# Linear attention stage: epsilon as a column of the denominator sum, numerators in PSUM, and k and q added apart on GpSimd

## The chip, the cores and the metric

The kernel runs on one core of a Trainium2 chip. The metric is the device time of one execution in microseconds (us). The engines are TensorE (PE in the rows; PEld its weight loads), VectorE (DVE), ScalarE (ACT), GpSimd (POOL) and the DMA queues.

## The reference

One transformer layer on x of (16, 256, 128) float32: a causal linear attention with 16 heads of 8, and then a mixture of 16 experts (top 1) with a shared expert, each between layer norms and residual additions. The change touches the attention alone:

```
q = elu((x @ Wq + bq)) + 1;  k = elu((x @ Wk + bk)) + 1;  v = x @ Wv + bv     # x layer-normed
def step(carry, qkv):                     # over the 256 tokens of a row
    s, z = carry
    q_i, k_i, v_i = qkv
    s = s + jnp.einsum('bhd,bhm->bhdm', k_i, v_i)
    z = z + k_i
    qs = jnp.einsum('bhd,bhdm->bhm', q_i, s)
    qz = jnp.einsum('bhd,bhd->bh', q_i, z)[..., None]
    return ((s, z), qs / (qz + 1e-06))
return values @ Wo + bo
```

## The kernel before

The 4096 tokens are 32 tiles of 128 tokens, a token to a partition. A row of the batch is two tiles, an even one (the first half) and an odd one; what an odd tile needs of its even neighbour is the carried state. No loop runs on the chip: each engine's queue is written out by `step1(t, u)`, tile after tile, and `wait_ge` on counting semaphores ties the queues together. An engine takes its queue strictly in order, so a wait holds all that stands behind it.

For tile t, in the order of the data:

- TensorE transposes the normed x (L1032), ScalarE copies it to SBUF (`xnT`, L535), TensorE projects it to q, k and v in one PSUM bank (L1044), two tiles ahead: the queue of step t holds the projection of t + 2.
- ScalarE makes the halves of elu + 1: `neg` (L550), `rl` (L551), `ex` (L553), and copies v to `vv` (L555).
- GpSimd adds the halves, `qk <- ex, rl`, 128x256 for q and k together (L446), and multiplies k by v for every head, `kv`, 128x1024 (L452).
- TensorE sums k over the tokens up to each one with the triangular matrix `upto` (L1013, called z here); in even tiles it also makes the state to carry (L1017); and it sums `kv` in the same way into a pair of PSUM banks, `ps_s[u % 2]` (L1025: two halves of 512 columns, each two passes, so four rows in the trace). These sums of tile t may start when `kv` of t is there and VectorE's `prod` of t - 2 has read the same banks.
- VectorE multiplies q by the summed k (`zq`, L721) and q by the summed `kv` (`prod`, L735, 128x1024), reduces both over the 8 values of a head (`den` L752, `num` L757), adds epsilon to `den` (even tiles, L762; odd ones together with the carried part, L766), adds the carried numerators in odd tiles (L771), takes the reciprocal (L730) and multiplies (`att`, L745). The reciprocal and `att` of t - 1 stand in step t: the order of a step is zq(t), carry(t) if even, reciprocal(t-1), prod(t), att(t-1), den(t), num(t), and then L762, or L766 and L771.
- TensorE transposes `att` of t - 2 in step t (L1038), ScalarE copies it (`attT`, L545), TensorE multiplies it by Wo (L1051 for the bias and L1053), ScalarE stores it (L558). In odd tiles TensorE also transposes q (L1034), ScalarE copies it (`qT`, L541), and TensorE multiplies it by the carried state (L1058).

`s_chain` ("attention_steps") counts VectorE's operations of this stage, 6 for each tile (`CH`). `Z_READ` and `S_READ` say behind how many of them `zq` (and the carry) and `prod` are done. `s_att` counts the `att` tiles. From tile 28 on, VectorE places three small steps of the next stage's layer norms behind each of its attention steps (`other`).

Of the kernel before, what the change touches and what calls it, by code (L numbers as in the profile page):

```python
# [24 lines left out]
ALU = mybir.AluOpType  # L25
ACT = mybir.ActivationFunctionType
AX = mybir.AxisListType.X
# [110 lines left out]
def build(nc, x, w_att, b_qkv, bo, w_ffn, gate_up, down, out):  # L138
# [29 lines left out]
    with ExitStack() as ctx:  # L168
# [56 lines left out]
        zq = sb("zq", [P, D])  # L225
        den = sb("den", [P, NH])
        rden = sb("rden", [P, NH])
        prod = sb("prod", [P, KVW])
# [75 lines left out]
        s_bias_rows = sem("bias_rows_written")  # L304
        s_norm1 = sem("norm1_ready")
# [6 lines left out]
        s_v = sem("v_ready")  # L312
        s_qk = sem("qk_ready")
# [60 lines left out]
        CH = 6  # L374
# [53 lines left out]
        def _(pool):  # L428
# [7 lines left out]
            nc.gpsimd.memset(bias_rows[:], 0.0).then_inc(s_bias_clear, 1)  # L436
            nc.gpsimd.memset(rows[:, NT:ST, :], 0.0).then_inc(s_zero, 1)
# [4 lines left out]
            def step1(t, u):  # L442
# [3 lines left out]
                nc.gpsimd.tensor_tensor(qk[:, u, :], ex[:, u % 2, :], rl[:, u % 2, :], ALU.add).then_inc(s_qk, 1)  # L446
                pool.wait_ge(s_qk, t + 1)
# [5 lines left out]
                                        k, v, ALU.mult).then_inc(s_kv, 1)  # L453
            run_steps(pool, step1, 0, 4, 28, NT, 8, 4)
# [193 lines left out]
        def _(dve):  # L648
# [63 lines left out]
            def step1(t, u, others=iter(()), between=3):  # L712
# [4 lines left out]
                multiplied = S_READ[u % 2]  # L717
                if live(t, NT):

                    dve.wait_ge(s_z, t + 1)  # L720
                    nc.vector.tensor_tensor(zq[:], ps_qkv[u % 2][:, 3 * D:4 * D], qk[:, u, 0:D],  # L721
                                            ALU.mult).then_inc(s_chain, 1)
                    other()
# [4 lines left out]
                if live(t - 1, NT):  # L728
                    dve.wait_ge(s_chain, CH * (t - 1) + S_READ[1 - u % 2] + 3)
                    nc.vector.reciprocal(rden[:], rden[:]).then_inc(s_recip, 1)  # L730
                    other()
                if live(t, NT):
# [3 lines left out]
                        prod[:].rearrange("p (h m d) -> p h m d", h=NH, m=HD),  # L736
# [4 lines left out]
                if live(t - 1, NT):  # L741
                    dve.wait_ge(s_recip, t)
                    dve.wait_ge(s_chain, CH * t)
# [6 lines left out]
                if live(t, NT):  # L750
                    dve.wait_ge(s_chain, CH * t + Z_READ[u % 2])
                    nc.vector.tensor_reduce(den[:], zq[:].rearrange("p (h d) -> p h d", h=NH), AX,  # L752
                                            ALU.add).then_inc(s_chain, 1)
                    other()
                    dve.wait_ge(s_chain, CH * t + multiplied)
# [4 lines left out]
                    dve.wait_ge(s_chain, CH * t + multiplied + 1)  # L760
# [456 lines left out]
```

## Time and profile before

| what | us |
|---|---|
| median of 3 runs (342.65 to 344.68) | 344.0 |
| the profiled execution | 344.77 |
| its span | 342.8 |
| attention stage, from the first `zq` to the last `att` | 24.3 to 150.9 |
| busy in the span: PE, DVE, ACT, POOL | 269.8, 286.7, 186.5, 192.5 |

All rows below come from the one profiled execution. A row of the timeline gives the start from the beginning of the span, the duration, the engine, the line of the kernel, the operation and what it writes and reads; "x4" merges four of a kind, and in brackets stands how long the engine was idle before and who released it. A matmul's end is modelled, so on TensorE the distance from start to start says more than the duration.

### The profile page before, as it was taken

How to read it: one execution, taken by the hardware profiler on the slowest of the kernel's cores; microseconds unless marked ns; L12 is line 12 of the kernel's file. 1: busy time of each engine (PE TensorE's matmuls, PEld its weight loads, DVE VectorE, ACT ScalarE, POOL GpSimd, SP SyncE). 2: the span in 40 equal slices, each digit the busy share in tenths (PEclk: the TensorE clock that was granted, in tenths of full speed). 3: DMA queues.
4: the chain of work that ended last, by engine and by line, in shares of the span. 5: the costliest groups of instructions: out<-in, count | busy, mean ns of one | idle time of the engine just before them, and what ended most of it. 6: DMA issues, size and time to landing. Idle time of an engine off the chain costs nothing. (4 is left out here: it accounts for less than half of the span.)

```text
span 342.8 us, 6291 instructions
## 1 busy us (share of the span) xinstructions
PE 269.8 (79%) x1481; PEld 186.0 (54%) x1481; DVE 286.7 (84%) x1138; ACT 186.5 (54%) x573; POOL 192.5 (56%) x221
## 2 busy tenths in 40 slices
PE   3439999999998995839888888875999999998000
PEld 1215555555554552524555555543999888988000
DVE  6996999999999999996899988740389999999930
ACT  2524666656564652447666664203899888885000
POOL 5155777786776773300055556760007888888870
PEclk9987999999999999876999999999899999999755
DMA  6999900000000000000011111227940111110000
GB/s 190 376 424 391 409 8 0 2 3 0 2 0 2 2 0 0 0 2 2 0 63 64 63 62 64 95 78 238 354 158 24 31 35 37 40 36 30 26 2 0
DMA packets 13684, 28.39 MB, mean 83 GB/s; under 512 B 1966, under 2 KB 10166, under 8 KB 12626
## 3 DMA queue, kind: packets, MB, share of 16 engines
q1 hardware_dynamic: 10464, 21.57, 17.2%
q0 software_dynamic: 3040, 6.37, 5.5%
q8 instruction: 13, 0.21, 0.3%
q14 instruction: 21, 0.17, 0.2%
q10 hardware_dynamic: 146, 0.07, 0.1%
HBM read 15.38 MB, written 13.60 MB: 85 GB/s over the span
## 5 line engine op out<-in xcount | busy, mean ns | idle before, releaser
L452 POOL TENSOR_TENSOR kv<-qk,vv 128x1024 f32<-128x1024 f32 x32 | 62.4, 1950 | 2.5
L1025 PE MATMUL banks<-kv,upto 128*128 128x512 f32 x128 | 62.6, 612 | 1.3 <-POOL kv L452 1.3
L1164 PE MATMUL banks<-xsT,w_now 128*128 128x128 f32 x376 | 52.6, 284 | 0.3 <-DVE hT_e L964 0.3
L497 POOL DMA_INDIRECT out<-rows,token_i x47 | 46.8, 996 | 9.9 <-issue 8.3
L446 POOL TENSOR_TENSOR qk<-ex,rl 128x256 f32<-128x256 f32 x32 | 23.3, 727 | 47.2 <-ACT ex L553 47.2
L1164 PEld LDWEIGHTS banks<-xsT,w_now 128*128 128x128 f32 x376 | 47.1, 197 | 0.9 <-issue 0.6
L479 POOL DMA_INDIRECT sorted_rows<-rows,slot_i x32 | 31.7, 990 | 25.8 <-DVE slot_i L821 17.7
L735 DVE TENSOR_TENSOR prod<-banks,qk 128x1024 f32<-128x1024 f32 x32 | 38.9, 1216 | 3.5 <-PE banks L1025 2.9
L757 DVE TENSOR_REDUCE num<-prod 128x128 f32<-128x1024 f32 x32 | 38.6, 1207 | 0.3 <-DVE den L752 0.3
L964 DVE TENSOR_TENSOR hT_e<-silu_e,banks 128x256 f32<-128x256 f32 x47 | 19.3, 412 | 18.8 <-ACT silu_e L640 15.3
L1044 PE MATMUL banks<-w_qkvo,xnT 128*128 128x384 f32 x64 | 28.7, 532 | 8.1 <-ACT xnT L535 3.9
L491 POOL TENSOR_TENSOR rows<-rows,yn 128x128 f32<-128x128 f32 x40 | 19.0, 475 | 27.5 <-DVE yn L956 25.8
L1025 PEld LDWEIGHTS banks<-kv,upto 128*128 128x128 f32 x128 | 22.9, 198 | 17.6 <-issue 16.1
L1172 PE MATMUL banks<-w_exp_down,hT_e 128*128 x188 | 29.6, 280 | 1.0 <-DVE rows L981 1.0
L630 ACT ACTIVATE xs<-rows 128x128 f32<-128x128 f32 x47 | 23.2, 494 | 11.5 <-SPq L421 11.5
L644 ACT COPY w_now<-w_exp 128x512 f32 x47 | 28.7, 610 | 0.0
L535 ACT COPY xnT<-banks 128x128 f32<-128x128 f32 x32 | 8.5, 264 | 34.3 <-PE banks L1032 20.0
L1172 PEld LDWEIGHTS banks<-w_exp_down,hT_e 128*128 128x128 f32 x188 | 24.7, 191 | 1.5 <-issue 1.4
L640 ACT ACTIVATE silu_e<-banks 128x256 f32<-128x256 f32 x47 | 18.0, 383 | 11.8 <-PE banks L1164 11.1
L1120 PE MATMUL banks<-w_ffn,hT 128*128 128x128 f32 x128 | 16.4, 281 | 9.5 <-DVE hT L831 9.5
L528 ACT ACTIVATE xn<-rows,nm,rs 128x128 f32<-128x128 f32 x32 | 16.4, 517 | 10.3 <-DVE nm L122 10.3
L1120 PEld LDWEIGHTS banks<-w_ffn,hT 128*128 128x128 f32 x128 | 14.9, 191 | 11.2 <-DVE hT L831 11.2
(161 smaller groups left out, 647.8 us busy)
## 6 DMA issues: line engine op xcount, KB each, us to landing
sorted_rows<-rows SPq DMA_DIRECT2D x3, 1950.0 KB, 13.4
rows<-sorted_rows SPq DMA_DIRECT2D x10, 520.0 KB, 6.3
w_exp<-in_gate_up SPq DMA_DIRECT2D x4, 1024.0 KB, 20.3
w_exp_down<-in_down SPq DMA_DIRECT2D x4, 512.0 KB, 20.4
rows<-in_x SPq DMA_DIRECT2D x1, 1024.0 KB, 11.0
rows<-sorted_rows SPq DMA_DIRECT2D x2, 390.0 KB, 4.7
rows<-in_x SPq DMA_DIRECT2D x1, 768.0 KB, 8.2
out<-rows,token_i POOLq DMA_INDIRECT x47
```

Source lines behind the costliest of these rows:

```text
L446: nc.gpsimd.tensor_tensor(qk[:, u, :], ex[:, u % 2, :], rl[:, u % 2, :], ALU.add).then_inc(s_qk, 1)
L452: nc.gpsimd.tensor_tensor(kv[:, u, :].rearrange("p (h m d) -> p h m d", h=NH, m=HD), k, v, ALU.mult).then_inc(s_kv, 1)
L479: nc.gpsimd.indirect_dma_start(out=sorted_rows, out_offset=bass.IndirectOffsetOnAxis(ap=slot_i[:, t:t + 1], axis=0), in_=rows[:, t, :], in ...
L497: nc.gpsimd.indirect_dma_start(out=out_rows, out_offset=bass.IndirectOffsetOnAxis(ap=token_i[:, j - 1:j], axis=0), in_=rows[:, j - 1, 0:D] ...
L644: nc.scalar.copy(w_now[:, u % 2, :], flat(w_exp[:, bass.ds(e, 1), :])).then_inc(s_wn, 1)
L735: nc.vector.tensor_tensor(prod[:].rearrange("p (h m d) -> p h m d", h=NH, m=HD), ps_s[u % 2][:].rearrange("p (h m d) -> p h m d", h=NH, m=HD),
L757: nc.vector.tensor_reduce(num[:], prod[:].rearrange("p (n d) -> p n d", d=HD), AX, ALU.add).then_inc(s_chain, 1)
L1025: ins = nc.tensor.matmul(ps_s[u % 2][:, cols], upto[:], kv[:, u, cols], start=True, stop=True)
L1044: nc.tensor.matmul(ps_qkv[u % 2][:, 0:3 * D], xnT[:, u % 2, :], w_qkv, start=True, stop=True).then_inc(s_qkv, 1)
L1120: ins = nc.tensor.matmul(into, hT[:, f, k * P:(k + 1) * P], w_d[:, f, :], start=f == 0, stop=f == FC - 1)
L1164: ins = nc.tensor.matmul(ps_gue[u % 2][:, c * P:(c + 1) * P], w_now[:, u % 2, c * P:(c + 1) * P], xsT[:, u % 2, :], start=True, stop=True)
L1172: ins = nc.tensor.matmul(ps_ye[u % 2][:, 0:D], hT_e[:, u % 2, c * P:(c + 1) * P], flat(w_exp_down[:, bass.ds(e, 1), c, :]), start=c == 0, ...
```

## The change

- `zq` gets a ninth column for each head, which GpSimd fills once with epsilon, and two buffers. The reduction to `den` covers nine values, so L762 goes and L766 becomes a plain addition. There are now 5 counted VectorE operations in an even tile and 6 in an odd one (`steps_before`).
- The numerators are reduced into the first 128 columns of the tile's own pair of PSUM banks (even tiles), or written there by the addition of the carried part (odd tiles); `att` reads them from PSUM. `prod` gets two buffers.
- Since the banks now hold the numerators until `att` has read them, the sums of `kv` for tile t wait for `att` of t - 2 and no longer for `prod` of t - 2.
- GpSimd adds the k half of `qk` first, then multiplies `kv`, then adds the q half. The z sums and `kv` wait for the k half (`s_k`); `zq`, the transpose of q and ScalarE's `neg` of t + 2 wait for the q half (`s_qk`).

```diff
-        CH = 6
+        def steps_before(t):
+            return 11 * (t // 2) + 5 * (t % 2)
...
+            nc.gpsimd.memset(zq[:, :, :, HD:HD + 1], EPS_DEN).then_inc(s_eps, 1)
...
-                nc.gpsimd.tensor_tensor(qk[:, u, :], ex[:, u % 2, :], rl[:, u % 2, :], ALU.add).then_inc(s_qk, 1)
-                pool.wait_ge(s_qk, t + 1)
+                nc.gpsimd.tensor_tensor(qk[:, u, D:2 * D], ex[:, u % 2, D:2 * D], rl[:, u % 2, D:2 * D], ALU.add
+                                        ).then_inc(s_k, 1)
+                pool.wait_ge(s_k, t + 1)
...
                 nc.gpsimd.tensor_tensor(kv[:, u, :].rearrange("p (h m d) -> p h m d", h=NH, m=HD),
                                         k, v, ALU.mult).then_inc(s_kv, 1)
+                nc.gpsimd.tensor_tensor(qk[:, u, 0:D], ex[:, u % 2, 0:D], rl[:, u % 2, 0:D], ALU.add).then_inc(s_qk, 1)
...
+                summed, summed_last = ps_s[u % 2][:, 0:D], ps_s[1 - u % 2][:, 0:D]
...
                     dve.wait_ge(s_z, t + 1)
+                    dve.wait_ge(s_qk, t + 1)
...
                     nc.vector.tensor_tensor(att[:, 1 - u % 2, :].rearrange("p (h m) -> p h m", h=NH),
-                                            num[:].rearrange("p (h m) -> p h m", h=NH),
+                                            summed_last.rearrange("p (h m) -> p h m", h=NH),
...
-                    nc.vector.tensor_reduce(num[:], prod[:].rearrange("p (n d) -> p n d", d=HD), AX,
+                    nc.vector.tensor_reduce(num[:] if u % 2 else summed, prod[:, u % 2, :].rearrange("p (n d) -> p n d", d=HD), AX,
...
-                    if u % 2 == 0:
-                        nc.vector.tensor_scalar(rden[:], den[:], EPS_DEN, None, ALU.add).then_inc(s_chain, 1)
+                    if u % 2:
...
+                        nc.vector.tensor_tensor(rden[:], ps_xT[:, 3 * D:2 * D + CW], den[:], ALU.add).then_inc(s_chain, 1)
...
-                        nc.vector.tensor_tensor(num[:], num[:], ps_xT[:, 2 * D:3 * D], ALU.add).then_inc(s_chain, 1)
+                        nc.vector.tensor_tensor(summed, num[:], ps_xT[:, 2 * D:3 * D], ALU.add).then_inc(s_chain, 1)
...
                     pe.wait_ge(s_kv, t + 1)
-                    at_least(pe, s_chain, CH * (t - 2) + S_READ[odd])
+                    at_least(pe, s_att, t - 1)
```

VectorE's queue over an even and then an odd tile, before (banks2 and banks4 are the two pairs for the sums, banks0 holds the z sums, banks6 the carried part):

```order
L745 TENSOR_TENSOR att<-num,rden 128x128 [waits att_transposed,attention_steps,denominator_inverted]
L752 TENSOR_REDUCE den<-zq 128x16 [waits attention_steps]
L757 TENSOR_REDUCE num<-prod 128x128 [waits att_ready,attention_steps]
L762 TENSOR_SCALAR rden<-den 128x16 [waits attention_steps]
L721 TENSOR_TENSOR zq<-banks0,qk 128x128 [waits z_summed]
L730 RECIPROCAL rden<-rden 128x16 [waits attention_steps]
L735 TENSOR_TENSOR prod<-banks4,qk 128x1024 [waits state_summed]
```

And after, the same place:

```order
L756 TENSOR_TENSOR att<-banks4,rden 128x128 [waits att_transposed,attention_steps,denominator_inverted]
L765 TENSOR_REDUCE den<-zq 128x16 [waits attention_steps]
L770 TENSOR_REDUCE banks2<-prod 128x128 [waits att_ready,attention_steps]
L730 TENSOR_TENSOR zq<-banks0,qk 128x16x8 [waits qk_ready,z_summed]
L741 RECIPROCAL rden<-den 128x16 [waits attention_steps]
L746 TENSOR_TENSOR prod<-banks4,qk 128x1024 [waits state_summed]
```

The epsilon operation is gone, `att` reads and the reduction writes PSUM, and `zq` has one more wait.

TensorE's queue from the sums of an even tile to those of the next odd one, before:

```order
L1025 MATMUL banks<-kv,upto 128x512 [waits attention_steps,kv_ready]
L1025 MATMUL banks<-kv,upto 128x512
L1032 MATMUL banks<-ident,xn 128x128 [waits xnT_ready,xn_ready,attention_steps]
L1038 MATMUL banks<-ident,att 128x128 [waits y_stored,att_ready]
L1044 MATMUL banks<-w_qkvo,xnT 128x384 [waits attention_steps,xnT_ready]
L1051 MATMUL banks<-bias_rows,ones_bf 128x128 [waits attT_ready]
L1053 MATMUL banks<-w_qkvo,attT 128x128
L1013 MATMUL banks<-qk,upto 128x128 [waits v_ready,qk_ready]
L1025 MATMUL banks<-kv,upto 128x512 [waits attention_steps,kv_ready]
```

And after:

```order
L1033 MATMUL banks<-kv,upto 128x512 [waits att_ready,kv_ready]
L1033 MATMUL banks<-kv,upto 128x512
L1040 MATMUL banks<-ident,xn 128x128 [waits xnT_ready,xn_ready,attention_steps]
L1047 MATMUL banks<-ident,att 128x128 [waits y_stored,att_ready]
L1053 MATMUL banks<-w_qkvo,xnT 128x384 [waits attention_steps,xnT_ready]
L1060 MATMUL banks<-bias_rows,ones_bf 128x128 [waits attT_ready]
L1062 MATMUL banks<-w_qkvo,attT 128x128
L1021 MATMUL banks<-qk,upto 128x128 [waits v_ready,k_ready]
L1033 MATMUL banks<-kv,upto 128x512 [waits att_ready,kv_ready]
```

Nothing changes place; the sums wait for `att` in place of a step of the chain, and z for the k half alone.

GpSimd's queue for two tiles, before and after:

```order
L446 TENSOR_TENSOR qk<-ex,rl 128x256 [waits elu_halves_ready]
L452 TENSOR_TENSOR kv<-qk,vv 128x1024 [waits v_ready,qk_ready]
L446 TENSOR_TENSOR qk<-ex,rl 128x256 [waits elu_halves_ready]
L452 TENSOR_TENSOR kv<-qk,vv 128x1024 [waits v_ready,qk_ready]
L446 TENSOR_TENSOR qk<-ex,rl 128x256 [waits elu_halves_ready]
```

```order
L451 TENSOR_TENSOR qk<-ex,rl 128x128 [waits elu_halves_ready]
L458 TENSOR_TENSOR kv<-qk,vv 128x1024 [waits v_ready,k_ready]
L460 TENSOR_TENSOR qk<-ex,rl 128x128
L451 TENSOR_TENSOR qk<-ex,rl 128x128 [waits elu_halves_ready]
L458 TENSOR_TENSOR kv<-qk,vv 128x1024 [waits v_ready,k_ready]
L460 TENSOR_TENSOR qk<-ex,rl 128x128
```

Two operations a tile become three, with the q half behind `kv`.

## Rows read from the trace of the kernel before

**Rows 1.** Windows: stretch, length, busy PE, PEld, DVE, ACT, POOL, granted clock, DMA.

```profile
60.00:100.00 40.00, 39.92 (x177) 23.03 (x177) 39.72 (x92) 24.86 (x98) 29.79 (x24) 1.00 0.01 1
```

**Rows 2.** Timeline of VectorE: `zq` of four odd tiles.

```profile
36.83 0.28 DVE L721 TENSOR_TENSOR zq<-banks,qk 128x128 f32<-128x128 f32 x1
...
100.53 0.28 DVE L721 TENSOR_TENSOR zq<-banks,qk 128x128 f32<-128x128 f32 x1
...
109.47 0.28 DVE L721 TENSOR_TENSOR zq<-banks,qk 128x128 f32<-128x128 f32 x1
...
116.32 0.28 DVE L721 TENSOR_TENSOR zq<-banks,qk 128x128 f32<-128x128 f32 x1
```

**Rows 3.** Timeline of TensorE over one pair of tiles.

```profile
100.74 0.27 PE L1032 MATMUL banks<-ident,xn 128*128 128x128 f32 x1
...
101.89 0.10 PEld L1051 LDWEIGHTS banks<-bias_rows,ones_bf 128*128 128x128 bf16 x1 [0.63 <-ACT attT L545]
...
102.95 1.88 PE L1025 MATMUL banks<-kv,upto 128*128 128x512 f32 x4
...
104.67 0.27 PE L1032 MATMUL banks<-ident,xn 128*128 128x128 f32 x1
...
106.09 1.88 PE L1025 MATMUL banks<-kv,upto 128*128 128x512 f32 x4
```

**Rows 4.** Timeline of VectorE over the same pair and the next step.

```profile
100.46 0.17 DVE L762 TENSOR_SCALAR rden<-den 128x16 f32<-128x16 f32 x1
...
100.94 1.22 DVE L735 TENSOR_TENSOR prod<-banks,qk 128x1024 f32<-128x1024 f32 x1
...
102.08 0.52 DVE L745 TENSOR_TENSOR att<-num,rden 128x128 f32<-128x128 f32 x1
...
104.57 0.24 DVE L730 RECIPROCAL rden<-rden 128x16 f32<-128x16 f32 x1
104.87 1.23 DVE L735 TENSOR_TENSOR prod<-banks,qk 128x1024 f32<-128x1024 f32 x1
...
106.01 0.28 DVE L745 TENSOR_TENSOR att<-num,rden 128x128 f32<-128x128 f32 x1
...
107.89 1.67 DVE L762 TENSOR_SCALAR rden<-den 128x16 f32<-128x16 f32 x1
```

**Rows 5.** Timeline of GpSimd over the same stretch: `kv`.

```profile
100.50 1.95 POOL L452 TENSOR_TENSOR kv<-qk,vv 128x1024 f32<-128x1024 f32 x1
...
103.76 1.95 POOL L452 TENSOR_TENSOR kv<-qk,vv 128x1024 f32<-128x1024 f32 x1
...
107.58 1.95 POOL L452 TENSOR_TENSOR kv<-qk,vv 128x1024 f32<-128x1024 f32 x1
```

**Rows 6.** Timeline at the end of the stage, GpSimd and VectorE.

```profile
131.00 1.95 POOL L452 TENSOR_TENSOR kv<-qk,vv 128x1024 f32<-128x1024 f32 x1
131.09 2.02 DVE L745 TENSOR_TENSOR att<-num,rden 128x128 f32<-128x128 f32 x1
```

**Rows 7.** One line each: ns min/median/max, first and last start.

```profile
L721 DVE TENSOR_TENSOR zq<-banks,qk x32: 276/283/292, 24.3 to 147.1; 128x128 f32<-128x128 f32 x32
L745 DVE TENSOR_TENSOR att<-num,rden x32: 272/282/2015, 31.6 to 150.6; 128x128 f32<-128x128 f32 x32
L446 POOL TENSOR_TENSOR qk<-ex,rl x32: 722/727/732, 16.2 to 138.0; 128x256 f32<-128x256 f32 x32
```

**Rows 8.** Timeline of the start: GpSimd, VectorE and TensorE.

```profile
16.97 1.95 POOL L452 TENSOR_TENSOR kv<-qk,vv 128x1024 f32<-128x1024 f32 x1
17.44 1.54 DVE L93 TENSOR_TENSOR scratch<-stats 128x28 f32<-128x28 f32 x1
...
18.97 1.98 PE L1025 MATMUL banks<-kv,upto 128*128 128x512 f32 x4 [1.29 <-POOL kv L452]
...
20.79 0.27 PE L1032 MATMUL banks<-ident,xn 128*128 128x128 f32 x1
```

**Rows 9.** One line: a 128x128 addition on GpSimd in a later stage.

```profile
L491 POOL TENSOR_TENSOR rows<-rows,yn x40: 442/477/502, 255.4 to 322.8; 128x128 f32<-128x128 f32 x40
```

More of the change, by code:

```diff
@@ L224, in build @@
         kv = sb("kv", [P, 4, KVW])
-        zq = sb("zq", [P, D])
+        zq = sb("zq", [P, 2, NH, HD + 1])
         den = sb("den", [P, NH])
         rden = sb("rden", [P, NH])
-        prod = sb("prod", [P, KVW])
+        prod = sb("prod", [P, 2, KVW])
         num = sb("num", [P, D])
@@ L304, in build @@
         s_bias_rows = sem("bias_rows_written")
+        s_eps = sem("denominator_eps_written")
         s_norm1 = sem("norm1_ready")
@@ L312, in build @@
         s_v = sem("v_ready")
+        s_k = sem("k_ready")
         s_qk = sem("qk_ready")
@@ L728, in step1 @@
                 if live(t - 1, NT):
-                    dve.wait_ge(s_chain, CH * (t - 1) + S_READ[1 - u % 2] + 3)
-                    nc.vector.reciprocal(rden[:], rden[:]).then_inc(s_recip, 1)
+                    dve.wait_ge(s_chain, steps_before(t - 1) + (4 if u % 2 else 5))
+                    nc.vector.reciprocal(rden[:], (den if u % 2 else rden)[:]).then_inc(s_recip, 1)
                     other()
@@ L735, in step1 @@
                     nc.vector.tensor_tensor(
-                        prod[:].rearrange("p (h m d) -> p h m d", h=NH, m=HD),
+                        prod[:, u % 2, :].rearrange("p (h m d) -> p h m d", h=NH, m=HD),
                         ps_s[u % 2][:].rearrange("p (h m d) -> p h m d", h=NH, m=HD),
@@ L750, in step1 @@
                 if live(t, NT):
-                    dve.wait_ge(s_chain, CH * t + Z_READ[u % 2])
-                    nc.vector.tensor_reduce(den[:], zq[:].rearrange("p (h d) -> p h d", h=NH), AX,
+                    dve.wait_ge(s_chain, steps_before(t) + Z_READ[u % 2])
+                    if t == 0:
+                        dve.wait_ge(s_eps, 1)
+                    nc.vector.tensor_reduce(den[:], zq[:, u % 2, :, :], AX,
                                             ALU.add).then_inc(s_chain, 1)
@@ L763, in step1 @@
                         other()
-                    else:
-                        dve.wait_ge(s_carried, t + 1)
-                        nc.vector.scalar_tensor_tensor(out=rden[:], in0=den[:], scalar=EPS_DEN,
-                                                       in1=ps_xT[:, 3 * D:2 * D + CW],
-                                                       op0=ALU.add, op1=ALU.add).then_inc(s_chain, 1)
-                        other()
-                        dve.wait_ge(s_chain, CH * t + multiplied + 2)
-                        nc.vector.tensor_tensor(num[:], num[:], ps_xT[:, 2 * D:3 * D], ALU.add).then_inc(s_chain, 1)
+                        dve.wait_ge(s_chain, steps_before(t) + multiplied + 2)
@@ L1007, in step1 @@
                 if live(t, NT):
-                    pe.wait_ge(s_qk, t + 1)
+                    pe.wait_ge(s_k, t + 1)
                     pe.wait_ge(s_v, t + 1)
@@ L1033, in step1 @@
                 if odd and live(t, NT):
+                    pe.wait_ge(s_qk, t + 1)
                     nc.tensor.transpose(ps_xT[:, D:2 * D], qk[:, u, 0:D], ident[:]).then_inc(s_q_t, 2)
@@ L1042, in step1 @@
                         pe.wait_ge(s_folded, 1)
-                    at_least(pe, s_chain, CH * t + Z_READ[odd])
+                    at_least(pe, s_chain, steps_before(t) + Z_READ[odd])
                     nc.tensor.matmul(ps_qkv[u % 2][:, 0:3 * D], xnT[:, u % 2, :], w_qkv,
@@ L1130, in _ @@
             pe.wait_ge(s_xnT, NT)
-            pe.wait_ge(s_chain, CH * NT)
+            pe.wait_ge(s_chain, steps_before(NT))
             step2(-1, 1)
-            pe.wait_ge(s_chain, CH * NT)
+            pe.wait_ge(s_chain, steps_before(NT))
             pe.wait_ge(s_y_out, NT)
```

15 lines of the change are left out of this document (9 added, 6 removed).

## The prediction

> **What bounds the kernel now.** I first cut the span into stretches and read each engine's busy time and the granted clock [rows 1]. From 60 to 100 us, the middle of the attention stage, TensorE is busy 39.92 of 40 us and VectorE 39.72 of 40, at the full granted clock (1.00, which is 2.4 GHz). Busy shares can't tell two full engines apart, so the timeline of one pair of tiles comes next: the program repeats every two tiles, an odd one and an even one. The odd `zq` starts at 36.83 and at 100.53 us, nine pairs later [rows 2]: 7.08 us for a pair.
>
> On TensorE [rows 3] the pair beginning at 100.74 is: transposes and the rest of the odd step until the k v sums (L1025, below "the sums") of the even tile start at 102.95, 2.21 us; their four passes until 104.67, 1.72; transposes, projection, output, z until the odd tile's sums at 106.09, 1.42; four passes until 107.81, 1.72. Sum 7.07 (the second four passes taken like the first). The only hole is a small one before L1051 at 101.89, whose row names `attT` of ScalarE. TensorE never waits for VectorE in this pair.
>
> VectorE's own row [rows 4]: the even `prod` starts at 104.87, 0.04 us behind the end of the sums (102.95 + 1.88). The step from the reciprocal (104.57, 0.24 long) to it is 0.30, while operations here start some 0.08 ahead of the end of the one before (`prod` 100.94 + 1.22 = 102.16, `att` 102.08), so that 0.16 to 0.2 would do. So VectorE waits about 0.1 us a pair for TensorE. Inside the pair it also loses 0.24: the odd `att` takes 0.52 instead of 0.28, and ends when GpSimd's `kv` (100.50 + 1.95 = 102.45) is through [rows 4, 5]. Since the pair's length is TensorE's, these 0.24 us are no loss of the kernel now; without them the 0.1 wait would be 0.34. That reading decides the forecast.
>
> Two stalls are different in kind, because they are too long to be absorbed. At 107.89 the 128x16 add of epsilon (L762), else 0.17 us long, takes 1.67: it begins 0.31 behind a `kv`, while at 100.46 it begins 0.04 ahead of one [rows 4, 5]. A short pause of VectorE just before had made it late. The pair is 8.94 long instead of 7.07 and the next 6.85 [rows 2]: net 1.65 us lost. At 131.09 `att` takes 2.02 behind a `kv` of 131.00 [rows 6]; VectorE is the bound there, since the norm steps of the next stage stand between the attention steps.
>
> **The change part by part.**
>
> *Epsilon.* 16 adds L762 leave VectorE. Start to start each costs 0.07 (100.46 to 100.53) [rows 4], 14 of them in steps paced by TensorE: nothing. Two (tiles 28 and 30) lie where VectorE is the bound: -0.14 at most. L766 becomes a plain add, equal. The `den` reduction reads 144 values instead of 128: with `att` 0.28 for 128 and `prod` 1.22 for 1024 [rows 4] about 1 ns a value, +0.02, hidden by VectorE's idle time. `zq` is now written in runs of 8 with a gap; no row shows such a write. Bounds 0 and +0.1, I take 0; at +0.1 it is hidden too. The held L762 at 107.89 is gone: **-1.65**, bounds -1.87 and -1.5. The memset of the column is 32 values on GpSimd at 1.8 us, far ahead of its first tile (its `kv` at 16.97): 0.
>
> *Numerators in PSUM.* `att` then has one SBUF input. The row shows that `att` with both inputs in SBUF is held behind `kv`; no operation with a PSUM input is (`zq` at 276 to 292 ns in all 32 cases, the one at 100.53 during a `kv`) [rows 2, 5, 7]. So the odd `att` falls from 0.52 to 0.28: off the path, 0. A PSUM write by VectorE is in no row; a PSUM input costs nothing visible (`zq` 283 against `att` 282 ns, medians) [rows 7]. For the write I bound 0 to +0.1 each, take 0; in the even step it falls into the time that VectorE idles anyway.
>
> The Trainium skill, "VectorE: DVE Perf Modes", section on the TRN2 errata, speaks against this: it gives a fixed 120 cycles for a PSUM source against 58 for SBUF, so `att` would be some 0.065 us longer (an estimate from that page), and 13 of them on the path below would add 0.8 us. The rows of this case (283 against 282 ns) do not show it, and I leave it out.
>
> *The wait that this brings.* The numerators of tile t-2 lie in the banks into which the sums of tile t go. The sums used to wait for `prod` of t-2; now they wait for `att` of t-2, which VectorE does only behind `prod` of t-1. Even tile: `att` (odd step) starts 102.08, would end 102.36, the sums start 102.95: free. Odd tile: `att` starts at 106.01 and ends at 106.29, but the sums start at 106.09 [rows 3, 4]. They must move behind it. How much an engine needs from a release: at the first tile the sums start at 18.97, 0.05 behind the end of `kv` (16.97 + 1.95), and the next instruction on TensorE starts 1.82 later instead of 1.72, since the weights are not loaded ahead [rows 8]. So the effective start is 106.29 + 0.05 + 0.10 = 106.44, **+0.35 a pair**. Bounds: +0.20 (no latency at all) and +0.38. Does something give it back? Everything behind the sums on TensorE's queue (transposes of xn, q and att, projection of tile t+2, then ScalarE's copies and the q, k, v of that tile) moves with them. `att` can't come earlier: it is `prod` (1.14) behind the end of the even sums, and these are TensorE's. The even half keeps 3.93 us (1.72 + 2.21). The new pair is 1.92 + 1.14 + 0.28 + 0.15 + 3.93 = 7.42. VectorE needs about 7.07 - 0.1 - 0.24 - 0.07 = 6.66 and waits. The odd tiles from 3 to 27 are 13: +4.55.
>
> *The halves on GpSimd.* k (128x128) is about 0.48 (the 128x128 add of L491) [rows 9] instead of the 0.73 of the whole `qk` [rows 7]: `kv` is ready 0.25 earlier. TensorE had the odd `kv` (103.76 + 1.95 = 105.71) 0.38 before it used it (106.09) [rows 3, 5], so nothing is won. q comes 0.56 behind `kv`, at about 106.0 here (105.71 - 0.25 + 0.56), for a `zq` of that tile which starts behind the L762 of 107.89; the transpose of q stands behind the sums in TensorE's queue, and ScalarE asks for q later still (its L550). GpSimd's queue becomes 0.48 + 1.95 + 0.48 + two gaps of 0.08 = 3.1 us a tile where the pair leaves 3.54 (7.07 / 2): it fits. 0. If q were late, `zq` and the projection behind it would be, at 0.1 a tile for each 0.1.
>
> *Start.* The norm chain of 28 tiles (L93 to L122) has small operations with two SBUF inputs, held while GpSimd works (L93 1.54 us behind the `kv` of 16.97) [rows 8]; ScalarE waits for its end. The first `kv` begins 0.25 earlier, but two more adds can hold a step. -0.2, bounds -0.5 and +0.5.
>
> *End of the stage, 127 to 151 us.* VectorE is the bound. It comes 0.2 earlier relative to TensorE. `att` at 131.09 is no longer held, but the norm steps L108 and L110 right behind it have two SBUF inputs and stand before the same `kv`: the first of them is held instead, so of 1.74 only some 0.3 is won. Together with the two L762: **-0.6**, bounds -2.2 (all 1.74 saved) and +1.5 (another small step held by a `kv`).
>
> *Sum.* +4.55 - 1.65 - 0.2 - 0.6 = +2.1. The profiled execution took 344.8 (span 342.8), 0.8 above the median 344.0 of the three; I read that as the held L762, which need not occur in each. The sum against the profiled one is 346.9, and the changed kernel has no such event, so its median should lie at it: **346.8 us**.
>
> **Rivals.**
> 1. *VectorE paces the pair* (0.14). For: 99% busy, its wait of 0.1 us is small and TensorE's ends are modelled. Then each pair gives back 0.24 + 0.07, 13 pairs 4.0, the two long stalls 3.4 and the start 0.2: 337.2. Against: TensorE has no hole in which it waits for VectorE [rows 3]. The Trainium skill, "SBUF — State Buffer", section on the two separate sides, states an exclusive lock between a VectorE operation with two SBUF inputs and a GpSimd operation; the held rows agree, and by it every attention step is freed. It is this rival's mechanism, but says nothing on who paces.
> 2. *The new wait costs its lower bound and the end its best* (0.24): 13 x 0.20 = 2.6, -1.65 - 2.2 - 0.2: 343.3; with 0.35 and the same end 345.3. No measurable change.
> 3. *More is held* (0.12): the small norm steps at start or end meet two further `kv`, 1.7 us each: 350.3; with one 348.6.
> 4. My forecast, sums behind `att`: 0.50, 346.0 to 347.6.
>
> That the change doesn't free `att` at all would alter little, since those 0.24 us are off the path.
>
> **How the numbers follow.** The other side of the forecast is rival 1, which decides if the sums of odd tiles turn out to start no later relative to `att` of the step before than now. 0.5% is 1.7 us, about what a measurement here can tell: faster means below 342.3, slower above 345.7. Faster: 0.14 and a quarter of rival 2, 0.20. Slower: 0.12 and most of 0.50, 0.54. Same: 0.26. Range 339.5 to 349.5; it leaves out the core of rival 1 and the far end of rival 3.
>
> **What the changed profile would show.** The odd `zq` 7.4 us apart (rival 1: 6.8 to 6.9); the first pass of the odd sums some 0.05 to 0.15 behind the end of `att`, with `att` as releaser; before `prod` some 0.3 to 0.4 us idle on VectorE; every `att` at 0.28; no long operation between 36 and 125 us; and around 131 us one L106, L108 or L110 held for 1.5 us or more. I am wrong if the pair stays at 7.07, if VectorE has no idle time in it, or if a PSUM write costs tenths of a us.

## The result, and the profile after

The changed kernel takes 350.5 us (median of four runs, 348.2 to 351.3) against 344.05 (342.65 to 344.68, four runs): ratio 1.018, interval 1.012 to 1.024. That is 6.4 us slower. The forecast was 346.8, 2.8 us slower. Its direction was right, its size was not, and 350.5 lies 1 us outside the range. The profiled execution took 348.18 (span 346.4, mean granted clock 0.935), the shortest of the four; the others took 349.97 to 351.29 at 0.909 to 0.930. All comparisons of traces below are of profiled executions, 348.18 against 344.77.

The middle of the attention stage first, by windows (columns as in [rows 1]):

```profile
60.00:100.00 40.00, 38.99 (x168) 22.43 (x169) 36.38 (x84) 23.60 (x91) 29.86 (x33) 1.00 0.00 1
```

TensorE was busy 39.92 of 40 us and is at 38.99, VectorE went from 39.72 to 36.38: both have holes now. The timeline of one pair shows where (start, us, engine, line, operation; in brackets the idle time before it and its releaser). The sums, L1025 of before, are L1033 here, `att` is L756, `prod` L746, `zq` L730, `kv` L458 and the two halves of `qk` L451 (k) and L460 (q).

```profile
61.06 1.88 PE L1033 MATMUL banks<-kv,upto 128*128 128x512 f32 x4
...
62.98 1.22 DVE L746 TENSOR_TENSOR prod<-banks,qk 128x1024 f32<-128x1024 f32 x1 [0.27 <-PE banks L1033]
...
64.12 0.28 DVE L756 TENSOR_TENSOR att<-banks,rden 128x128 f32<-128x128 f32 x1
...
64.52 0.30 PEld L1033 LDWEIGHTS banks<-kv,upto 128*128 128x128 f32 x2 [0.35 <-issue]
64.55 1.96 PE L1033 MATMUL banks<-kv,upto 128*128 128x512 f32 x4 [0.18 <-DVE att L756]
...
65.66 0.28 DVE L730 TENSOR_TENSOR zq<-banks,qk 128x128 f32<-128x128 f32 x1
...
66.34 0.27 PE L1040 MATMUL banks<-ident,xn 128*128 128x128 f32 x1
66.54 1.22 DVE L746 TENSOR_TENSOR prod<-banks,qk 128x1024 f32<-128x1024 f32 x1 [0.45 <-PE banks L1033]
...
73.15 0.28 DVE L730 TENSOR_TENSOR zq<-banks,qk 128x128 f32<-128x128 f32 x1
```

These answer to [rows 2 to 4]. The odd `zq` starts at 65.66 and 73.15: 7.49 us a pair, where it was 7.07. The even sums end at 62.94, `prod` starts 0.04 later, `att` ends at 64.40, and the odd sums, which before started 0.08 behind the *start* of `att`, now load their weights 0.12 behind its *end* and name it as releaser. VectorE idles 0.27 and 0.45 before its two `prod`, since everything on TensorE has moved back.

Over the whole stage, by groups of instructions of the page (busy us, mean ns | idle us before them, and what ended it):

```profile
L1033 PE MATMUL banks<-kv,upto 128*128 128x512 f32 x128 | 67.3, 652 | 9.4 <-DVE att L756 8.5
...
L746 DVE TENSOR_TENSOR prod<-banks,qk 128x1024 f32<-128x1024 f32 x32 | 39.1, 1223 | 11.9 <-PE banks L1033 11.9
```

Before, the same two lines of the page read

```profile
L1025 PE MATMUL banks<-kv,upto 128*128 128x512 f32 x128 | 62.6, 612 | 1.3 <-POOL kv L452 1.3
...
L735 DVE TENSOR_TENSOR prod<-banks,qk 128x1024 f32<-128x1024 f32 x32 | 38.9, 1216 | 3.5 <-PE banks L1025 2.9
```

8.5 us of waiting for `att` are new, and the sums themselves are 4.7 us longer in all (67.3 against 62.6). About 1 us of the second is the 1.96 against 1.88 of the sums that wait in the middle; most of the rest lies at the end of the stage. Timeline of the changed kernel there, VectorE, GpSimd and the sums:

```profile
131.60 1.22 DVE L746 TENSOR_TENSOR prod<-banks,qk 128x1024 f32<-128x1024 f32 x1
...
133.19 1.96 POOL L458 TENSOR_TENSOR kv<-qk,vv 128x1024 f32<-128x1024 f32 x1
133.36 1.80 DVE L106 TENSOR_TENSOR scratch<-scratch 128x4 f32<-128x4 f32 x1
135.09 0.28 DVE L756 TENSOR_TENSOR att<-banks,rden 128x128 f32<-128x128 f32 x1
...
135.51 3.75 PE L1033 MATMUL banks<-kv,upto 128*128 128x512 f32 x4 [3.37 <-DVE att L756]
...
139.30 1.23 DVE L746 TENSOR_TENSOR prod<-banks,qk 128x1024 f32<-128x1024 f32 x1 [1.16 <-PE banks L1033]
...
148.12 3.48 PE L1033 MATMUL banks<-kv,upto 128*128 128x512 f32 x4 [3.13 <-DVE att L756]
```

and the windows of that place in the changed kernel, TensorE's granted clock being the column before the last two:

```profile
134.00:141.00 7.00, 5.49 (x10) 2.54 (x11) 5.70 (x16) 0.43 (x2) 1.55 (x2) 0.51 0.00 0
```

The norm step L106 is held behind a `kv`, as the prediction said some such step would be. But `att` of tile 27 is queued right behind it, and the sums of tile 29 now wait for that `att`. TensorE stands still for 3.37 us, and then its four passes take 3.75 instead of 1.88: the granted clock is 0.51, so 1.2 GHz, the lower of its two levels. The same happens again at 148.12 for tile 31, where the residual addition L880 (1.91 us from 143.49) and further steps of the next stage stand ahead of `att`. Before, the sums of tile 29 ran at 129.52 in 1.88 us, ahead of the held `att` of [rows 6]. The granted clock falls at the end of the stage before the change too (0.76 over the same 134 to 141 us, 0.60 from 135.7 to 138.7), where TensorE has had 0.44 us of work in 4.3 us (131.4 to 135.7); what is new is that two tiles' sums run inside the low clock from their start and that VectorE waits for the first of them: `prod` at 139.30 has 1.16 us of idle time ahead of it.

Marks along the stage, in us of the two profiled executions:

| | before | after | difference |
|---|---|---|---|
| `zq` of tile 0 | 24.32 | 24.27 | -0.05 |
| `zq` of tile 3 | 36.83 | 35.69 | -1.14 |
| tile 3 to tile 27 (12 pairs) | 86.56 | 89.90 | +3.34 |
| tile 27 to tile 31 | 23.69 | 25.56 | +1.87 |
| tile 31 to the end of the last `att` | 3.84 | 4.05 | +0.21 |
| rest of the span | 191.9 | 191.2 | -0.7 |

The -1.14 can't be put down to the change: between 20 and 36 us the granted clock was 0.79 in one and 1.00 in the other, and among the kernels below (apart from "halves alone", whose add is held there) tile 3 starts at 34.9 to 37.4 without a pattern. The rest of the span, which is identical code, lies between 190.5 and 194.8 in the profiles of all kernels below.

### The profile page after: what moved, and what is told of

The parts are those of the page before. It is cut to its first block and busy times, and to the rows that moved or that the text cites. A ratio compares the mean times of both kernels' runs of the same rounds, so it can differ in the third digit from the quotient of the medians.

```text
span 346.4 us, 6357 instructions
## 1 busy us (share of the span) xinstructions
PE 276.8 (80%) x1481; PEld 187.8 (54%) x1481; DVE 282.3 (81%) x1122; ACT 186.2 (54%) x573; POOL 197.5 (57%) x254
## 5 line engine op out<-in xcount | busy, mean ns | idle before, releaser
L1033 PE MATMUL banks<-kv,upto 128*128 128x512 f32 x128 | 67.3, 652 | 9.4 <-DVE att L756 8.5
L458 POOL TENSOR_TENSOR kv<-qk,vv 128x1024 f32<-128x1024 f32 x32 | 62.4, 1951 | 2.5
L746 DVE TENSOR_TENSOR prod<-banks,qk 128x1024 f32<-128x1024 f32 x32 | 39.1, 1223 | 11.9 <-PE banks L1033 11.9
L451 POOL TENSOR_TENSOR qk<-ex,rl 128x128 f32<-128x128 f32 x32 | 14.5, 454 | 46.8 <-ACT ex L560 46.8
L1033 PEld LDWEIGHTS banks<-kv,upto 128*128 128x128 f32 x128 | 23.8, 206 | 29.6 <-issue 25.0
L964 DVE TENSOR_SCALAR yn<-rows,rstd,nmean 128x128 f32<-128x128 f32 x47 | 19.8, 420 | 0.0
```

Source lines behind the costliest of these rows:

```text
L458: nc.gpsimd.tensor_tensor(kv[:, u, :].rearrange("p (h m d) -> p h m d", h=NH, m=HD), k, v, ALU.mult).then_inc(s_kv, 1)
L746: nc.vector.tensor_tensor(prod[:, u % 2, :].rearrange("p (h m d) -> p h m d", h=NH, m=HD), ps_s[u % 2][:].rearrange("p (h m d) -> p h m d" ...
L964: nc.vector.tensor_scalar(yn[:, u, :], flat(rows[:, i, D:2 * D]), rstd3[:, parity, u:u + 1], nmean3[:, parity, u:u + 1], ALU.mult, ALU.add ...
L1033: ins = nc.tensor.matmul(ps_s[u % 2][:, cols], upto[:], kv[:, u, cols], start=True, stop=True)
```

## The experiments

The theory after the result: the sums' new wait for `att` of tile t-2 costs all of the loss, 0.42 us a pair and about 2 us at the end of the stage; epsilon column, PSUM as a place for numerators, and the halves on GpSimd add nothing to it. Rivals: the PSUM operands are slow; the halves on GpSimd delay something; the end is late for another reason. "Middle" is `zq` of tile 3 to tile 27, "end" is tile 27 to tile 31, both from the profiled execution. The medians stand against the kernel before as it ran on the same chip beside them: 343.58 (first four kernels), 344.23 (next four), 344.02 (last four).

| kernel | median us | ratio, interval | pair | middle | end |
|---|---|---|---|---|---|
| before | 344.05 | 1 | 7.07 | 86.56 | 23.69 |
| changed | 350.49 | 1.018, 1.012 to 1.024 | 7.49 | 89.90 | 25.56 |
| wait alone | 349.82 | 1.021, 1.011 to 1.030 | 7.49 | 91.12 | 25.52 |
| passes of the sums swapped | 343.38 | 0.997, 0.992 to 1.001 | 7.07 | 85.13 | 23.92 |
| numerators in SBUF | 343.54 | 1.001, 0.998 to 1.005 | 7.07 | 85.12 | 23.31 |
| qk whole | 350.21 | 1.019, 1.011 to 1.026 | 7.49 | 89.90 | 24.91 |
| last tiles in SBUF | 347.08 | 1.008, 1.004 to 1.012 | 7.49 | 89.90 | 24.47 |
| swapped, last in SBUF | 342.31 | 0.995, 0.991 to 0.999 | 7.07 | 85.11 | 24.05 |
| epsilon column alone | 343.33 | 0.997, 0.993 to 1.001 | 7.09 | 85.52 | 23.53 |
| halves alone | 361.55 | 1.048, 1.039 to 1.057 | 8.44 | 101.51 | 23.90 |
| attT first, before | 343.92 | 0.999, 0.995 to 1.002 | 7.07 | 86.47 | 24.36 |
| attT first, changed | 346.42 | 1.007, 1.003 to 1.010 | 7.32 | 87.93 | 25.57 |
| attT first, numerators in SBUF | 339.52 | 0.985, 0.980 to 0.990 | 6.90 | 83.15 | 23.33 |
| attT first, swapped, last in SBUF | 340.52 | 0.988, 0.983 to 0.993 | 6.90 | 83.25 | 24.04 |

**The wait alone**, put into the kernel before, where it is not needed (the numerators are in SBUF there):

```diff
-                    at_least(pe, s_chain, CH * (t - 2) + S_READ[odd])
+                    at_least(pe, s_att, t - 1)
```

> The kernel before with one line changed: TensorE's sums of tile t wait for att of t-2 instead of prod of t-2; everything else, numerators in SBUF and the epsilon step included, stays. Theory (the new wait is what costs): the pair of tiles goes from 7.07 to about 7.49 us as in the changed kernel, VectorE idles before prod, and the time is 348 to 352. At the end of the stage the sums of tile 29 wait behind the held att and the clock falls, as in the changed kernel. Rival (PSUM operands or the halves of GpSimd cost): pair within 0.05 of 7.07 and time within 1 us of before.

Measured +6.2 us, the same as the whole change within the intervals. Its rows in the timeline read like those of the changed kernel:

```profile
64.22 0.28 DVE L745 TENSOR_TENSOR att<-num,rden 128x128 f32<-128x128 f32 x1
64.65 1.96 PE L1025 MATMUL banks<-kv,upto 128*128 128x512 f32 x4 [0.19 <-DVE att L745]
```

and so does its end: L106 held for 1.80, 25.52 us from tile 27 to 31. Neither PSUM nor the halves are in this kernel, so neither is needed for the loss. One thing was not expected: `att` has both inputs in SBUF and yet always takes 0.28 in the middle. The wait has shifted VectorE against GpSimd: the `att` that was held before begins at 67.78 here, and the `kv` ahead of it (65.79 + 1.95) is over at 67.74. One L762 is held here too (at 111.03, 1.68), which makes the middle 91.12.

**The passes of the sums swapped.** The numerators lie in the first bank of a pair of banks. So the second half of the sums can go first, under the old wait, and only the first half waits for `att`:

```diff
-                    at_least(pe, s_att, t - 1)
-                    for half in range(2):
+                    at_least(pe, s_chain, steps_before(t - 2) + S_READ[odd] if t >= 2 else 0)
+                    for half in (1, 0):
+                        if half == 0:
+                            at_least(pe, s_att, t - 1)
```

> The changed kernel with the two halves of the sums in the other order: the half whose bank holds no numerators is summed first and waits only for prod of t-2, the other half waits for att of t-2. Theory (wait): the first half (0.86 us) covers the end of att, which came 0.2 us behind the old start; pair back to 7.05 to 7.10; no TensorE idle in front of the sums between 36 and 125 us; 345 or less; the end of the stage still pays. Rival: pair stays at 7.4 to 7.5.

The loss is gone and the pair is back at 7.07. The sums (L1035 here) start 0.08 behind the start of `att`, without a wait, while the numerators are still written to PSUM and read from there:

```profile
63.51 0.28 DVE L756 TENSOR_TENSOR att<-banks,rden 128x128 f32<-128x128 f32 x1
63.59 1.88 PE L1035 MATMUL banks<-kv,upto 128*128 128x512 f32 x4
```

That rules out the PSUM operands as a cost: everything of the change but the position of the wait is in this kernel.

A miss: I expected the end still to pay, and it takes 23.92, as before the change. L106 is held for the same 1.80 (at 129.07), and TensorE still waits for the `att` behind it, but with half of the sums already done:

```profile
131.12 1.12 PE L1035 MATMUL banks<-kv,upto 128*128 128x512 f32 x2 [2.42 <-DVE att L756]
```

The half that is left takes 1.12 us, and the next `prod` finds it finished.

**Numerators in SBUF**, with the old wait, and the rest of the change kept:

```diff
-                summed, summed_last = ps_s[u % 2][:, 0:D], ps_s[1 - u % 2][:, 0:D]
+                summed, summed_last = num[:], num[:]
...
-                    at_least(pe, s_att, t - 1)
+                    at_least(pe, s_chain, steps_before(t - 2) + S_READ[odd] if t >= 2 else 0)
```

> The changed kernel with the numerators back in SBUF and the sums waiting for prod of t-2 again; the epsilon column and GpSimd's halves stay. Theory (wait): pair 7.05 to 7.10, odd att held again to about 0.5 us, no held step at 107.89 since L762 is gone; total 342 to 344. Rival (halves or epsilon column cost): pair above 7.2.

The time is that of before. A miss: I expected the odd `att` to be held again, at some 0.5. It takes 0.28. With the half of k alone ahead of it, `kv` starts earlier: 0.54 behind the even sums (67.23 and 66.69), where it was 0.81 (103.76 and 102.95 in [rows 3, 5]). The `kv` that used to hold `att` is nearly over when `att` begins:

```profile
60.16 1.95 POOL L458 TENSOR_TENSOR kv<-qk,vv 128x1024 f32<-128x1024 f32 x1
...
62.68 0.28 DVE L756 TENSOR_TENSOR att<-num,rden 128x128 f32<-128x128 f32 x1
...
63.98 1.95 POOL L458 TENSOR_TENSOR kv<-qk,vv 128x1024 f32<-128x1024 f32 x1
65.82 0.28 DVE L756 TENSOR_TENSOR att<-num,rden 128x128 f32<-128x128 f32 x1
```

The one at 65.82 is the odd `att`: 0.11 us of the `kv` of 63.98 (until 65.93) are left, where 0.37 were left in [rows 4, 5] (102.45 less 102.08). Against the changed kernel this one is 7.0 us faster by the medians; the traces give 4.8 in the middle and 2.25 at the end, together 7.0. So the price of the wait is known in both places.

**qk whole**, one addition of q and k ahead of `kv` again, the rest as changed:

```diff
-                nc.gpsimd.tensor_tensor(qk[:, u, D:2 * D], ex[:, u % 2, D:2 * D], rl[:, u % 2, D:2 * D], ALU.add
-                                        ).then_inc(s_k, 1)
+                nc.gpsimd.tensor_tensor(qk[:, u, :], ex[:, u % 2, :], rl[:, u % 2, :], ALU.add).then_inc(s_qk, 1)
...
-                nc.gpsimd.tensor_tensor(qk[:, u, 0:D], ex[:, u % 2, 0:D], rl[:, u % 2, 0:D], ALU.add).then_inc(s_qk, 1)
...
-                    pe.wait_ge(s_k, t + 1)
+                    pe.wait_ge(s_qk, t + 1)
```

> The changed kernel with qk added whole ahead of kv, as before; epsilon column and numerators in PSUM stay. Theory (wait): pair 7.45 to 7.5 as in the changed kernel, since kv is not what TensorE waits for; total within 1.5 us of the changed kernel. Rival (the halves cost): pair falls below 7.3.

Same time, same pair as the changed kernel, and at the end the same picture: L106 held for 1.80, sums of 3.64 us behind it, `prod` 1.19 us late. (The end is 24.91 and not 25.56; its L878, the L880 of the changed kernel, takes 1.09 instead of 1.91.) The halves are not what costs here.

**The last tiles in SBUF.** Tiles from 26 on keep their numerators in SBUF, and the sums of tiles 28 to 31 have the old wait:

```diff
+                summed = ps_s[u % 2][:, 0:D] if t < 26 else num[:]
...
-                    at_least(pe, s_att, t - 1)
+                    if t - 2 < 26:
+                        at_least(pe, s_att, t - 1)
+                    else:
+                        at_least(pe, s_chain, steps_before(t - 2) + S_READ[odd])
```

> The changed kernel, but tiles 26 to 31 keep their numerators in SBUF and the sums of tiles 28 to 31 wait for prod of t-2 as before. Theory (the second part of the loss is the same wait where VectorE is the bound: att of 27 stands behind a held norm step, TensorE idles 3.4 us and its clock halves): pairs 7.49 up to 125 us, then from the zq of tile 27 to that of 31 23.3 to 23.9 us instead of 25.56, total about 2 us below the changed kernel, 348 to 349. Rival (the end is slower for another reason): still 25 or more.

The middle is unchanged to the hundredth. L106 is held just the same, but no sums stand behind it now (timeline of this kernel):

```profile
131.22 1.88 PE L1037 MATMUL banks<-kv,upto 128*128 128x512 f32 x4
132.61 1.80 DVE L106 TENSOR_TENSOR scratch<-scratch 128x4 f32<-128x4 f32 x1
134.34 0.28 DVE L757 TENSOR_TENSOR att<-num,rden 128x128 f32<-128x128 f32 x1
```

They run ahead of the held step and in 1.88 us, and over 134 to 141 us the granted clock is 0.76, as in the kernel before, where the changed one has 0.51:

```profile
134.00:141.00 7.00, 3.83 (x13) 2.84 (x14) 6.38 (x19) 2.11 (x8) 1.66 (x4) 0.76 0.00 0
```

The end takes 24.47, 1.1 less than in the changed kernel but more than the 23.3 to 23.9 expected. By medians 3.4 us are won (2 expected), but a gain of 1.1 is at the edge of what the two intervals allow, so scatter can account for the difference. Of the 1.2 us that its end is longer than in "numerators in SBUF", 0.4 lies in the first pair (12.24 against 11.81): the sums of tile 27 wait for tile 25, which this kernel still keeps in PSUM. What the rest consists of was not settled.

**Both remedies together**, swapped passes and the last tiles in SBUF:

> Both remedies: halves of the sums in the other order and SBUF numerators from tile 26 on. Theory: pair 7.07, end 23.3 to 23.9, total 342.5 to 343.5, a little below the kernel before because no epsilon step can be held. Rival: above 344.

342.3 us, 0.5% under before, pair 7.07. Its end (24.05) is a little above the 23.3 to 23.9 expected and no better than with the swap alone (23.92).

**The epsilon column alone**, in the kernel before (nothing in PSUM, qk whole):

> The kernel before with the epsilon column alone: qk whole, numerators in SBUF, sums wait for prod. Theory: pair 7.07, since TensorE paces it; the odd att is held to 0.5 us as before; no held epsilon step; 342.5 to 344. Rival (the column pays for itself on VectorE): pair 6.9 or below.

No measurable difference, no held add, pair 7.08 to 7.10. With qk whole and numerators in SBUF the odd `att` is held again, and at the end of the stage it meets a whole `kv`:

```profile
64.91 1.95 POOL L457 TENSOR_TENSOR kv<-qk,vv 128x1024 f32<-128x1024 f32 x1
66.48 0.53 DVE L754 TENSOR_TENSOR att<-num,rden 128x128 f32<-128x128 f32 x1
```

Beside "numerators in SBUF", which differs from this kernel only in the halves, this separates the two causes: the half of k, by starting `kv` 0.27 earlier, is enough to free `att` of its hold; PSUM operands are not needed for it.

**The halves alone**, in the kernel before, with its 16 adds of epsilon (L766 here):

> The kernel before with GpSimd's halves alone: k half, kv, q half; epsilon step, SBUF numerators and the old wait stay. Following the timeline, kv then starts 0.25 us earlier relative to ScalarE and the epsilon step (0.04 ahead of kv before) starts behind it and is held up to 1.8 us in every even tile: pair about 8.4 and total about 360. Rival (the order on GpSimd does not matter as long as TensorE paces): pair 7.07, total 343 to 345.

361.6 us, 17 more than before. `kv` begins earlier, and so just ahead of an add that used to slip in before it:

```profile
61.75 1.95 POOL L454 TENSOR_TENSOR kv<-qk,vv 128x1024 f32<-128x1024 f32 x1
61.97 1.75 DVE L766 TENSOR_SCALAR rden<-den 128x16 f32<-128x16 f32 x1
...
70.40 1.95 POOL L454 TENSOR_TENSOR kv<-qk,vv 128x1024 f32<-128x1024 f32 x1
70.44 1.94 DVE L766 TENSOR_SCALAR rden<-den 128x16 f32<-128x16 f32 x1
```

Each even tile now loses it: 8.44 us a pair, as the expectation had it, and 8.66 in the one pair that holds the add of 70.44. In [rows 4, 5] the add began 0.04 ahead of `kv` and took 0.17; here at 70.44 it begins 0.04 behind and takes 1.94. By themselves the halves are the dearest part of the change; in this kernel they can only be had together with the epsilon column, which removes that add.

**attT first.** The last four kernels look for what else bounds the pair. ScalarE copies `qT` ahead of `attT` in odd tiles, and TensorE has its only regular hole where it waits for `attT` [rows 3]. The two blocks are exchanged, without any other edit:

```diff
-                if u % 2 and live(t, NT):
-                    act.wait_ge(s_q_t, t + 1)
-                    at_least(act, s_carried, t - 1)
-                    nc.scalar.copy(qT[:], ps_xT[:, D:2 * D]).then_inc(s_qT, 2)
                 if live(t - 2, NT):
                     act.wait_ge(s_att_t, t - 1)
                     at_least(act, s_y, t - 2)
                     nc.scalar.copy(attT[:], ps_o[:, 0:D]).then_inc(s_attT, 1)
+                if u % 2 and live(t, NT):
+                    act.wait_ge(s_q_t, t + 1)
+                    at_least(act, s_carried, t - 1)
+                    nc.scalar.copy(qT[:], ps_xT[:, D:2 * D]).then_inc(s_qT, 2)
```

> The kernel before with ScalarE's two copies of odd tiles in the other order: attT ahead of qT. TensorE's only hole in a pair, about 0.19 us in front of the output product, waits for attT. Theory (TensorE paces): the hole shrinks by up to 0.16 and the pair to 6.9, but with its held odd att VectorE needs 6.97, so it ends at 6.95 to 7.0 and VectorE becomes the bound: 341.5 to 343.5. Rival (TensorE is not the pace): 7.07 stays.

A miss: on the kernel before it changes nothing. The hole did shrink, from 5.4 us in 60 to 100 us to 3.6 (groups of that stretch, before and then this kernel):

```profile
L1051 PEld LDWEIGHTS banks<-bias_rows,ones_bf 128*128 128x128 bf16 x11 | 1.1, 95 | 5.4 <-ACT attT L545 5.4
```

```profile
L1051 PEld LDWEIGHTS banks<-bias_rows,ones_bf 128*128 128x128 bf16 x11 | 1.0, 95 | 3.6 <-ACT attT L541 3.6
```

But a delay of the same size has appeared in the even step (timeline of this kernel):

```profile
61.29 0.30 DVE L726 TENSOR_TENSOR carry<-banks,head_mask 128x144 f32<-128x144 f32 x1
...
61.73 0.88 PE L1044 MATMUL banks<-w_qkvo,xnT 128*128 128x384 f32 x2
...
64.93 1.23 DVE L735 TENSOR_TENSOR prod<-banks,qk 128x1024 f32<-128x1024 f32 x1
66.07 0.52 DVE L745 TENSOR_TENSOR att<-num,rden 128x128 f32<-128x128 f32 x1
```

The projection L1044 may start only when VectorE's `carry` is done, since both touch the same banks. Here `carry` ends at 61.59 and L1044 starts at 61.73, 0.31 behind L1032 and 0.88 long; in the kernel before it ends at 104.66, L1044 starts at 104.89, 0.22 behind L1032, and is 0.81 long. So there is a second path of the pair that goes through both engines: `carry`, L1044, the odd sums, the odd `prod` (64.93, 0.04 behind the sums), the held odd `att`, and the rest of VectorE's step up to the next `carry`. It is as long as TensorE's own, 7.07, and with the hole made smaller it sets the pair. The 0.24 us of the held `att` lie on it. So before the change the two paths were equal to less than 0.1 us, and a gain on TensorE alone brings nothing.

The same exchange in the changed kernel, where VectorE has 0.7 us of idle time a pair:

> The changed kernel with the same swap on ScalarE. The path of its pair (even sums, prod, att, odd sums, the odd half of TensorE) goes through the hole, so theory: 7.49 - 0.16 = 7.33, and 2 us less in all, 347.5 to 349. Rival (the pair is set by something beside that path): 7.49 stays.

7.32 a pair and 4.1 us less than the changed kernel by the medians; the traces show 2.0 of them, in the middle, and 2.0 was expected. The two intervals allow both. Here TensorE and the wait set the pair, no `att` is held, and the hole on TensorE counts.

And with the numerators in SBUF, halves and epsilon column kept:

> Numerators in SBUF with the old wait, epsilon column, halves of qk, and attT ahead of qT. In that kernel no att was held in the pairs, so VectorE needs about 6.66: theory pair 6.90 to 6.93, total 341 to 342, below the kernel before by 0.6 to 0.9%. Rival: att gets held again since the pair is shorter, 7.0 or more.

339.5 us, 4.5 less than before and 11 less than the changed kernel: the lowest of all, with a pair of 6.90. With both remedies in place of the numerators in SBUF it is 340.5, the same pair and 0.7 more at the end; the two intervals overlap:

> Halves of the sums in the other order, SBUF numerators from tile 26 on, epsilon column, halves of qk, and attT ahead of qT: pair 6.90 to 6.93; total 340.5 to 341.5, below the kernel before and the changed kernel. Rival: no shorter than 7.07.

In no kernel here does PSUM as a place for the numerators bring anything that SBUF does not.

## Why the prediction was wrong in size

*What held.* TensorE paces the pair, not VectorE (rival 1: 6.8 to 6.9 a pair; it is 7.49). The even sums run free, the odd ones wait for `att`, with it as releaser. `prod` waits 0.27 and 0.45 (said: 0.3 to 0.4). Every `att` takes 0.28; no long operation lies between 36 us and the end of the middle, so the held L762 of 107.89 is gone. L106 is held at the end. The halves add nothing to the cost (whole qk: 350.2), and an operation of VectorE into or out of PSUM costs nothing that counts: the reduction of 1024 takes 1.22 us into PSUM and 1.21 into SBUF, `att` from PSUM 281 ns where it was 282 from SBUF. The Trainium skill, "VectorE: DVE Perf Modes", errata section, gives a PSUM source a higher fixed cost than an SBUF source; I had left that out of the sum, and these rows do not show it. One reading was luckier than it looks: that the held `att` is off the path is true only because a second path, with it, is no longer than TensorE's own ("attT first").

*Term 1, the wait, +0.35 a pair: +0.42.* I took 0.05 as the time from a release to the sums, from one row of the start, where they wait for GpSimd, plus 0.10 for weights not loaded ahead. Measured: `att` ends at 64.40, the weights load at 64.52, and L1040 starts at 66.34, which with 1.72 us of passes is a start at 64.62. That is 0.22 behind the end of `att` instead of 0.15, and beyond my upper bound of +0.38. Over the twelve pairs of the middle it makes +0.8.

*Term 2, the end of the stage, -0.6, or -0.25 with the wait of the thirteenth pair, which lies there: +2.1* (1.87 + 0.21 of the marks). This is the step that failed. I followed `att` into the place where VectorE is the bound, said that a norm step would be held there instead, and priced it at what VectorE saves. I did not carry the new wait there. In the middle, the wait costs what TensorE loses against an `att` that is on time; at the end `att` stands behind 1.8 us of held norm step, and the sums, which before went ahead of all that, stand behind `att`. TensorE does nothing for 3.4 us, the granted clock behind that is 0.51, and the late sums take twice their time. The kernel with the wait alone has the same end (25.52), the one with numerators in SBUF has 23.31 although its L106 is held for the same 1.80: so it is the wait and not the held step. No run separates waiting from clock within the 2.25, but rows give an estimate. In "numerators in SBUF" `prod` of tile 29 follows its `zq` at once, and L880 is shorter:

```profile
132.70 0.28 DVE L730 TENSOR_TENSOR zq<-banks,qk 128x128 f32<-128x128 f32 x1
...
133.05 1.16 DVE L746 TENSOR_TENSOR prod<-banks,qk 128x1024 f32<-128x1024 f32 x1
...
137.18 1.26 DVE L880 TENSOR_TENSOR rows<-rows,ya 128x256 f32<-128x256 f32 x2
```

In the changed kernel `zq` starts at 137.70 and `prod`, held up for 1.16, at 139.30. Sums of 1.96 us from 135.51 would have ended at 137.47, ahead of that `zq`. So by this estimate the 1.16 us are there because the sums ran at the low clock: about half of the 2.25. Another 0.65 is L880 (1.91 against 1.26, each beside a `kv`; 1.09 to 1.91 in the kernels with the wait), and 0.30 the first pair (12.11 against 11.81). My upper bound of +1.5 thought of another held step and not of this.

*Term 3, the start, -0.2.* `zq` of tile 0 came 0.05 earlier, within the bounds. The norm chain went as followed: L93 at 17.67 held for 1.27 instead of 1.54.

*Term 4, from the sum to the median.* +2.1 on the profiled 344.77 gave 346.9; the profiled execution of the changed kernel is 348.18, 1.3 more: +0.8 and +2.3 by the two terms above, less 1.0 at the start, 0.7 in the rest of the span and 0.2 outside of it (1.2, and 0.1 of rounding). Its median is another 2.3 higher. I had set a sum made against one profiled execution equal to a median, with the reason that the held L762 (-1.65) was what put it above its own. That credit does not show clearly in the medians: the kernels without the wait and without the held add ("passes swapped", "numerators in SBUF", "epsilon column alone") lie at 343.3 to 343.5 against 343.6 and 344.2 of before, a gain of 0.0 to 0.9, while their traces are 1.2, 1.8 and 1.2 shorter in middle and end together. For two of the three the interval has room for the 1.2; for "numerators in SBUF" (0.998 to 1.005) it has none for 1.8. That the add is rarely held is not likely: the other two traces of kernels in which it stands at its old place hold it too, in the same pair ("wait alone" at 111.03 for 1.68, "attT first, before" at 107.05 for 1.85). What gives the credit back stays open. Without it the sum at the median would be +7.0 for the wait, less a few tenths, and the result is +6.4.

*The chances.* The rival that the end is worse (3, held norm steps, 348.6 or 350.3) came nearest in time, for another reason than it gave.

## What to carry to other kernels

When a result is put into the buffer that the next producer writes, the producer waits for the last reader instead of the first: price that wait in each stage apart, above all where the reader's engine is the bound and has other work queued ahead of it. If the buffer has parts, let the producer do the free part first: exchanging the two halves gave back all 7 us here. And where two paths are within 0.1 us of each other, shortening one brings nothing (attT first: 0) until the other is shorter as well (numerators in SBUF with attT first: 6.90 a pair instead of 7.07, 4.5 us under before).

## What the runs showed of the hardware

- From the end of an operation of VectorE to the load of weights that waits for it 0.12 us; until the waiting matmuls are effectively under way 0.22 (64.40, 64.52, 64.62 in the changed kernel).
- Whether a small operation is held by GpSimd is decided within less than 0.1 us: the 128x16 add, begun 0.04 ahead of a `kv` it took 0.17, begun 0.04 behind it 1.94. A shift of 0.27 us on GpSimd made 17 us of it (halves alone). The add has one tensor input and a constant, and is held like an operation with two inputs. That agrees with the Trainium skill, "SBUF — State Buffer", section on the two separate sides, where an operation in a 2-port mode takes the shared ports as well; whether the add runs in such a mode no row here shows.
- `att` at 65.82 ("numerators in SBUF") ran in 0.28 though a `kv` lasted until 65.93 by the profile, while `att` at 66.48 ("epsilon column alone") took 0.53 beside a `kv` until 66.86, so it ended 0.28 behind 66.73: the last 0.1 us of the profiled `kv` held nothing.
- After 3.4 us in which TensorE did nothing, its next four passes took 3.75 us instead of 1.88, at a granted clock of 0.51. In "wait alone" and "qk whole" the same place reads 3.65 us of nothing and then 3.75 and 3.64.
